# Identity transposes in the waits of the last attention body, row maxima ahead of probability copies there, and half of the high-part copies of the expert tiles moved from VectorE to ScalarE

## What is computed

```
h = tokens(x); h = concat([h, txt])
h = h + linear_attention(layernorm(h))             # no softmax
h = layernorm(h) -> block:
  qkv = ln(h) @ in_w.T + in_b;  12 heads of 16
  attn = softmax(q @ k.T / 4);  x = x + (attn @ v) @ out_w.T + out_b
  x = x + gelu(x @ mlp_w1 + b1) @ mlp_w2 + b2      # 192 -> 768 -> 192
  xm = ln(x);  gates = softmax(top2(xm @ gate_w.T + gate_b))
  x = x + sum over the 2 chosen of 4 experts of gate * (gelu(xm @ exp_w1[e] + b) @ exp_w2[e] + b)
```

## Time and profile before

| | us |
|---|---|
| median of 3 runs | 1282.54 |
| lowest and highest run | 1279.87, 1289.48 |
| the profiled execution | 1290.99 |
| its span, first to last instruction | 1289.2 |
| mean granted clock of TensorE | 0.99 |

### The profile page before, as it was taken

How to read it: one execution, slowest core, us unless ns; L and a number is a source line. 1 busy time by engine, 2 the same in 40 slices (tenths; PEclk the granted TensorE clock), 3 DMA queues, 4 the chain that set the end, 5 groups by cost and what they waited for, 6 DMA issues and landing times.

```text
span 1289.2 us, 28372 instructions
## 1 busy us (share of the span) xinstructions
PE 1199.4 (93%) x9874; PEld 1022.5 (79%) x9874; DVE 968.6 (75%) x2677; ACT 692.8 (54%) x1630; POOL 410.7 (32%) x397
## 2 busy tenths in 40 slices
PE   7899999999999999999997899999998999999994
PEld 6677777777777777777776799998887889988993
DVE  5677788777877788778866678787777787888783
ACT  1356555565555555565565754555543556555551
POOL 2111011011101011011100137877558455445444
PEclk9999999999999999999999999999998999999998
DMA  2572022211222012211400524446566567766662
GB/s 106 146 187 66 15 57 63 57 38 34 64 56 64 15 57 62 58 31 41 104 9 10 211 52 85 88 80 181 133 152 186 140 168 181 178 163 160 176 162 29
DMA packets 95387, 124.51 MB, mean 97 GB/s; under 512 B 9382, under 2 KB 87591, under 8 KB 91343
## 3 DMA queue, kind: packets, MB, share of 16 engines
q1 hardware_dynamic: 71743, 102.48, 26.6%
q0 software_dynamic: 23568, 21.06, 10.6%
HBM read 70.68 MB, written 52.83 MB: 96 GB/s over the span
## 4 chain that ended last, share of the span: by engine, by line
PE 56%; DVE 14%; issue 12%; POOL 7%; ACT 5%; DMA 4%; DVEq 0%; POOLq 0%; another core or an unknown queue 0%; SPq 0%; ACTq 0%
PE PS L1619 44%; PE PS L1622 12%; DMA out<-YO,ids 3%; POOL expert_rows L732 3%; DVE K L1178 2%; POOL out L769 2%; DVE st L1090 1%; DVE rec L1200 1%; ACT GF L980 1%; ACT XAT L787 1%; DMA consts<-in_attn_const 1%; POOL out L720 1%; DVE ZS L1148 1%; DVE CN L1201 1%; DVE CNT L1206 1%
## 5 line engine op out<-in xcount | busy, mean ns | idle before, releaser
L1619 PE MATMUL PS<-w2r,GH 128*120 (+1 forms) x828 | 247.7, 362 | 2.9 <-DVE GL L1347 1.6
L659 POOL TENSOR_TENSOR rs<-ve,minus_half 128x3 f32<-128x3 f32 (+1 forms) x80 | 58.7, 734 | 554.5 <-DVE ve L1095 554.5
L769 POOL DMA_INDIRECT out<-YO,ids x94 | 161.0, 1713 | 156.6 <-DVE flag L1560 74.9
L980 ACT ACTIVATE GF<-PS,b1c 128x480 f32<-128x480 f32 (+1 forms) x216 | 138.8, 642 | 132.7 <-PE PS L1619 113.6
L1619 PE MATMUL PS<-w2r,GL 128*120 (+1 forms) x828 | 208.0, 251 | 0.0
L812 ACT ACTIVATE PX<-PS,nb 128x165 f32<-128x165 f32 x576 | 176.5, 416 | 48.3 <-DVE nb L1166 46.6
L1619 PE MATMUL PS<-XH,w1r 128*128 128x480 f32 (+1 forms) x432 | 169.2, 394 | 14.5 <-ACT GF L980 6.5
L1619 PEld LDWEIGHTS PS<-w2r,GH 128*120 128x120 f32 x828 | 150.2, 181 | 6.5 <-DVE GL L1347 4.6
L1619 PEld LDWEIGHTS PS<-w2r,GL 128*120 128x120 f32 x828 | 152.4, 184 | 0.0
L1171 DVE COPY PT<-PS 128x384 f32<-128x384 f32 x144 | 80.2, 557 | 89.6 <-PE PS L1622 86.2
L1622 PE MATMUL PS<-ident,PX 128*128 128x128 f32 x864 | 130.4, 281 | 7.2 <-ACT PT L787 5.9
(11 more groups left out here) (270 smaller groups left out, 2310.0 us busy)
## 6 DMA issues: line engine op xcount, KB each, us to landing
w1r<-expert_w_parts SPq DMA_DIRECT2D x25, 1536.0 KB
expert_rows<-empty SPq DMA_DIRECT2D x45, 369.4 KB, 5.8
RT<-expert_rows SPq DMA_DIRECT2D x22, 369.4 KB
X<-x_scratch SPq DMA_DIRECT2D x11, 360.0 KB, 7.0
out<-X POOLq DMA_DIRECT2D x11, 360.0 KB, 5.6
XP<-in_patches SPq DMA_DIRECT2D x32, 108.0 KB
H<-in_txt SPq DMA_DIRECT2D x16, 192.0 KB, 3.9
out<-H SPq DMA_DIRECT2D x16, 192.0 KB
```

Source lines behind the costliest of these rows:

```text
L659: nc.gpsimd.tensor_tensor(rs[:, k - 1, 0:n], ve[:, k - 1, 0:n], eps_half[:, 0:n], ALU.pow).then_inc(rstd_ready[k - 1], 1)
L769: nc.gpsimd.indirect_dma_start(out[:, :], bass.IndirectOffsetOnAxis(ap=ids[:, i, t:t + 1], axis=0), YO[:, i % 2, t, :], None, bounds_check ...
L980: nc.scalar.activation(GF[:, m % 3, 0:n], PS[:, 2 + m % 2, 0:n], ACT.Gelu, bias=bias, scale=1.0).then_inc(gelu_ready, 1)
L1619: return nc.tensor.matmul(o, l, r, start=start, stop=stop)
```

## The change

Three edits. In the last attention body alone, TensorE gets 8 identity transposes ahead of `contexts(i, 0)`, 3 ahead of `normed_T(i, 0)` and 9 ahead of `project(i)`. There too, DVE takes the maxima of units 1, 2 and 3 ahead of the copies of groups 0, 2 and 4 instead of behind them. And in all 25 expert tiles ACT copies the high part of blocks 0, 2 and 4 right after their gelus, while DVE keeps the copies of blocks 1, 3 and 5 and all six low parts, and waits for `high_ready` before an even one.

```diff
@@ ScalarE, turn
             for m in range(KH):
                 gelu(base, m, b1c[:, bass.ds(e + 1, 1), m:m + 1].rearrange("p a b -> p (a b)"), rows_of(i + 1))
+                if m % 2 == 0:
+                    n = rows_of(i + 1)
+                    act.wait_ge(gelu_ready, base + m + 1 + 2)
+                    copy(GH[(i + 1) % 2][:, m, 0:n], GF[:, m % 3, 0:n]).then_inc(high_ready, 1)
@@ VectorE, body
+            if lin and core:
                 probsT(i, 0)
                 maxima(i, 1)
                 probsT(i, 2)
                 maxima(i, 2)
                 probsT(i, 4)
                 maxima(i, 3)
+            elif core:
+                maxima(i, 1)
+                probsT(i, 0)
+                maxima(i, 2)
+                probsT(i, 2)
+                maxima(i, 3)
+                probsT(i, 4)
@@ VectorE, row_hidden
             for m in ms:
-                dve.wait_ge(gelu_ready, base + m + 1 + 2)
-                steps.link(cp(GH[at][:, m, 0:n], GF[:, m % 3, 0:n]))
+                if m % 2 == 0:
+                    dve.wait_ge(high_ready, GROUPS * KH + i * (KH // 2) + m // 2 + 1)
+                else:
+                    dve.wait_ge(gelu_ready, base + m + 1 + 2)
+                    steps.link(cp(GH[at][:, m, 0:n], GF[:, m % 3, 0:n]))
@@ TensorE, body
             if core:
+                if not lin:
+                    keep_running(6, 8)
                 contexts(i, 0)
                 contexts(i, 1)
                 contexts(i, 2)
+                if not lin:
+                    keep_running(6, 3)
                 normed_T(i, 0)
...
             if core:
+                if not lin:
+                    keep_running(6, 9)
                 project(i)
```

## The result

| | before | after |
|---|---|---|
| median, 12 runs each | 1282.55 us | 1279.05 us |
| lowest, highest | 1278.97, 1289.48 | 1276.23, 1283.73 |
| profiled execution | 1290.99 | 1281.36 |

What follows compares the result with a forecast made beforehand. TensorE was taken as the bound in later expert turns, DVE in the first ones. The terms -1.1 - 1.6 - 2.2 + 1.9 = -3.0 us took the median of 1282.54 to 1279.5 us, range 1273 to 1287.

Steps and rivals of the forecast that it cites:

- maxima first: Last attention body: maxima ahead of DVE's copies let the exponentials start earlier, -1.1 us (bounds 0 and -1.7).
- transposes: Last attention body: transposes in TensorE's waits keep the clock up for the projection, -1.7 + 0.1 = -1.6 us.
- first turns, to tile 5: First expert turns, where DVE is the bound: ACT's copies relieve DVE, -2.2 us (bounds 0 and -4.0).
- later turns, tiles 5 to 9 and 9 to 22: Later expert turns, TensorE without a gap: odd gelus come late behind copies, 0.09 us a turn, +1.9 us.
- tail: Three half tiles at the end: no effect, as POOL still has two adds to start after DVE's last flag.
- the walk: First expert turns, gain followed along: 0.8 us by tile 0's end, 1.5 at TensorE's wait, 2.2 to 2.4 at `lex`.
- fifth block: Sign in the first expert turn: TensorE no longer waits at the fifth block of `up`; the wait was 1.26 us.
- 21 turns: Later expert turns: the 0.09 us loss counted in each of 21 turns, +1.9 us in all.
- The rival of POOL's chain: Kernel's end: POOL's chain sets it, the +1.9 is hidden and -4.9 counts, 1277.6 us; chance 0.18.
- the distance from flag to add hardly grows: Argument against POOL's chain setting the end: from DVE's flag to POOL's add, over 20 tiles, as if following TensorE's pace.
- The stretch from 973 to 1006: Expert turns where TensorE idled 5.0 us at a clock of 0.84 in the profile before, which the prediction couldn't explain.
- The rival that it clears: Stretch from 973 to 1006 us goes away: -4.7, with the sum's -3.0 it is -7.7, 1274.8 us; chance 0.06.

Runs made afterwards that it cites:

- second execution of the kernel before: The kernel before, unchanged, timed and profiled again: median 1283.15 us, ratio 1.0000.
- experiment 5: The kernel after with the maxima back behind the copies, the 20 identity transposes kept: 1280.42 us, ratio 0.9973 to the kernel before.
- experiment 4: The kernel after without the 20 identity transposes: 1278.97 us, ratio 0.9967 to the kernel before.
- experiment 8: The kernel after with ACT's copy of each even block behind the next gelu instead of ahead of it: ratio 0.9976 to the kernel before.
- experiments 11 and 12: 11: the kernel after, unchanged, again, ratio 0.9962; 12: the kernel after with ACT's copies in tiles 0 to 7 only, 0.9942; both to the kernel before.
- experiments 3: The kernel before with only the experts' edit (ACT copies blocks 0, 2, 4), attention as before: 1281.53 us, ratio 0.9987 to the kernel before.

## Why the prediction was right, and where it wasn't

The total was right: -3.0 us forecast, -3.5 measured (by the interval -2.3 to -5.8). That it was so near is partly luck, since larger misses of its terms cancel. The terms, against the second execution of the kernel before:

| term | forecast | stages |
|---|---|---|
| maxima first | -1.1 | -1.3 |
| transposes | -1.6 | -1.67 (without them the clock fell in three executions of four) |
| MLP (no edit) | 0 | -0.4 |
| first turns, to tile 5 | -2.2 | -1.25 |
| later turns, tiles 5 to 9 and 9 to 22 | +1.9 | -1.6 and +0.7 |
| tail | 0 | +1.3 |

These stages sum to -4.2; the two profiled executions stand 0.9 us apart only, since the one of the kernel after had lost 3.3 us by 677 us, ahead of all that was changed.

**Maxima first.** The mechanism was right, with 1.29 us at the exponentials of unit 3 for the 1.1.

**Transposes.** Right: the size of the clock's loss (1.7 us), their cost (0.1 forecast, none measured), and that they count for the clock, which experiment 5 and the ten executions with them show. What stays open is experiment 4, where the clock stayed up without them. If the order of the maxima was enough for it, the two edits remove the same stall and their sum would count it once; one execution can't show that.

**First turns.** The mechanism and the walk hold, though TensorE still waited 0.30 us at the fifth block where I had said it would not: TensorE's wait came 1.29 us earlier where I said 1.5, `lex` 2.0 (against the second execution of before, 965.58) where I said 2.2 to 2.4. The step that missed is that all of this reaches TensorE: from tile 0 to 5 only 1.25 us did.

**Later turns.** The mechanism is right (experiment 8) and so is its price, 0.10 us for 0.09. The step that failed is "21 turns": I let all be steady turns with TensorE full. In three of them, those of tiles 5 to 7, DVE was still late with the plan, and there the copies gain 1.7 us; in three later ones TensorE had waited 0.1 to 0.3 us at the head of the turn, and that is gone too.

**The tail.** "Nothing" was wrong. The rival of POOL's chain had the right mechanism, and its effect is the other way round from what I priced: it doesn't hide a loss, it keeps part of the gain. The prediction's argument against it, that the distance from flag to add hardly grows, was no argument: POOL's last add there waited 3.01 us for a DMA and not for a flag. At tile 22 the kernel after is 5.6 us ahead of the second execution of before (counted from the last but one projection), at the end 4.2. It isn't so in every execution. From tile 22 to the end 45.2 and 44.3 us were read in the two executions of experiments 11 and 12, where the long turns had held TensorE back and the chain was TensorE's, and 49.0 to 50.6 in the others with all adds, without a pattern that follows the edits.

**The stretch from 973 to 1006.** The rival that it clears was priced from the window, as if its 33 us were two turns. The two turns took 20.66 and 18.33 us, and the long turns cost 9.7 us in all and not 4.7. And they stood in the profiled execution, not in the median: clearing them takes nothing from 1282.54, so that nothing led to 1274.8 us.

**Where the gains of the attention part go** stays open: alone it gave 1.0 us of 3.0 in the median, and beside the experts part (experiments 3 and 4) 2.6. And the long turns behind 973 us are unexplained: engines wait there for each other with no work in between, at a time when POOL scatters without a pause. They come in both kernels, in five of the 14 executions; POOL scatters like this in executions without them too, so that alone is not the cause.

## What to carry to other kernels

Before two edits are summed, ask whether they remove the same wait, and run each alone. When one run says that a piece is worthless, look at what the engine did just ahead of the place, and count the executions on both sides: here ten with the filler kept the clock, three of four without it lost it, and the one that didn't is easily taken for proof. Moving work to an idle engine pays only where the relieved engine is the late one, and even then it costs where the new step stands ahead of something that a third engine waits for, also further down the same queue; giving it only to the turns that need it did best here, by an uncertain margin. Read the chain of waits up to its last piece before you price a gain upstream: where the end is a chain of landings, a gain reaches it only in part. And profile a kernel more than once before a stretch of it is explained.

## What the runs showed of the hardware

Identity transposes kept TensorE's clock up: with 20 of them in the waits the 12 matmuls behind took 2.22 us in ten executions of ten. Without them the same wait of 1.11 us left the same matmuls at 3.70 to 3.90 us in three executions and at 2.22 in one, and TensorE had been busy for 7.06 and 7.07 of the 10 us ahead in either case, so the wait and what stands just ahead of it don't decide alone. The landing of a tile's last adds is a piece of 3.7 us in the chain of the tail, where no weights are loaded any more (the last load is issued at 1234.89), and of 7.2 and 7.3 us for the two full tiles ahead of that. The waits of POOL for them, of the kernel after:

```profile
1231.90 1.59 POOL L769 DMA_INDIRECT out<-YO,ids  x1 [6.28 <-DMA out<-YO,ids]
1256.37 1.59 POOL L769 DMA_INDIRECT out<-YO,ids  x1 [3.00 <-DMA out<-YO,ids]
```
